# Linear attention with an expert-choice MLP: how 12 of 16 blocks of normed rows are turned

## Chip, cores and metric

The kernel runs on one core of one Trainium2 chip. Its time is device microseconds (us) from start to end of one execution; lower is better. Below, "rows" are tokens, "turned" means transposed.

## What is computed

x is (2, 4096, 512), fp32. Cut to what matters:

```python
xn = layernorm(x)                          # per row of 512
q, k, v = split(xn @ W_qkv + b_qkv)        # 16 heads of 32 columns
q, k = relu(q), relu(k)                    # times cos and sin of the position
kv   = einsum('bhld,bhle->bhde', k_cos, v) # and the same for sin
ctx  = (q_cos @ kv_cos + q_sin @ kv_sin) / (norm + 1e-4)
attn = ctx @ W_out + b_out
probs = softmax(xn @ choice_w.T)           # 8 experts, each takes its best 1024 rows of a batch
ffn  = scatter_add(gain * (silu(rows @ w1[e]) @ w2[e]))   # rows = the chosen rows of xn
out  = x + attn + ffn
```

## The kernel before

The program is written engine by engine; each engine runs its own list in order, and semaphores tie them together. SP (SyncE) issues nearly all loads and stores. There are three stages.

**Projections**, twice (once per batch), 8 blocks of 512 rows each, in four tiles (t) of 128 rows. For block n, VectorE (DVE) norms the rows of block n + 1 in two halves of two tiles (`norm_half`, lines 690 to 724): statistics (L693 to L699), a square root on ScalarE (ACT, L508), a Newton step (L704 to L713), then L719 writes the normed rows into the buffer `xn`. SP stores them to a DRAM table `normed` (L346), from which the experts later gather rows. TensorE (PE) turns each 128x512 tile of `xn` with four 128x128 transposes into a PSUM bank (`turn_x`, L1177), ACT copies it to `xT_hi` in a rounded fp32 form (L515), and DVE subtracts to get the rest `xT_lo` (`turned_lo`, L729). Every product is three matmuls (hi\*hi, lo\*hi, hi\*lo: L1161 to L1163). PE's order in a block: the query products of 512 rows (`q_half`, `q_rest`), then for each tile the value product `v_of` (with the router's 8 columns), the key product `k_of`, and `kv`, which adds keys x values of the tile before into PSUM. The transposes of block n + 1 stand between these: tiles 0 and 3 behind `v_of`, tiles 1 and 2 behind `k_of`. DVE answers each tile with `v_out` (L871 to L884), `k_out` (L891), `turned_lo`, `k_low` (L896); ACT with `turned_hi` and `k_high` (L566).

x comes in through one buffer, `xq`, that is the upper half of `xo`; the lower half is used for the first block's second half and, in the next stage, for output tiles. So the load of a half (L305) waits until the half before has been normed.

At the start SP loads, in this order: two halves of x, two tables, the query weights, the router's rows, the value weights, biases, the key weights (L310, each 1 MB and on 128 partitions). ACT and DVE split each part in hi and lo (L539, L554; L830, L847) before they go on to the first block. After block 1's halves are stored, SP loads W_out, and GpSimd (POOL) splits it (L389, L391).

**Attention**, 32 tiles per batch, with the search for each expert's chosen rows beside it; at the end of batch 0 PE turns the four tiles of batch 1's first block. **Experts**, 8 times 4 units of 512 gathered rows: here the rows already come in pieces of 128 numbers and are turned by DVE in 32x32 blocks (`rows_turn`, L790), and w1 is loaded by four loads of 32 partitions each (L331).

Of the kernel before, what the change touches and what calls it, by code (L numbers as in the profile page):

```python
# [32 lines left out]
P = 128  # L33
# [8 lines left out]
BLK = 512  # L42
# [71 lines left out]
def build(nc, x, w_qkv, b_qkv, w_out, b_out, choice_w, w1, w2, consts, bits, out, scratch):  # L114
# [6 lines left out]
    with ExitStack() as ctx:  # L121
# [31 lines left out]
        with ExitStack() as early:  # L153
# [26 lines left out]
            probE = sb("probE", [P, E, NT])  # L180
            probT = sb("probT", [P, 2, P])
            mark = sb("mark", [P, 2, P])
# [13 lines left out]
        xq, x_first = xo[:, 2:4, :], xo[:, 0:2, :]  # L196
# [51 lines left out]
        x_in, xn_ready = sem("x_in"), sem("xn_ready")  # L248
# [44 lines left out]
        def _(sp):  # L293
# [5 lines left out]
            def store_normed(j, s):  # L299
                sp.wait_ge(xn_ready, j * TPB + (2 * s + 2))  # L300
                sp.dma_start(normed[bass.ds(j * BLK + 2 * s * P, 2 * P), :].rearrange("(t p) d -> p t d", p=P),
                             xn[:, 2 * s:2 * s + 2, :]).then_inc(xn_stored[s], 16)

            def load_x(row):
                sp.dma_start(xq, xf[bass.ds(row, 2 * P), :].rearrange("(t p) d -> p t d", p=P)  # L305
                             ).then_inc(x_in, 16)

            def load_weights(part):
                src = w_out if part == O else w_qkv[:, part * D:(part + 1) * D]
                sp.dma_start(raw_weights(part), src.rearrange("(k p) d -> p k d", p=P)).then_inc(w_in[part], 16)  # L310


            load_x(0)
            sp.dma_start(x_first, xf[2 * P:4 * P, :].rearrange("(t p) d -> p t d", p=P)).then_inc(x_in, 16)
# [3 lines left out]
            sp.dma_start(ch_rows, choice_w[:, :]).then_inc(ch_in, 16)  # L318
# [20 lines left out]
            for b in range(B):  # L339
                def next_block(nxt):  # L340
                    src = nxt * BLK
                    for s in range(2):
                        sp.wait_ge(xn_ready, nxt * TPB + 2 * s)
                        load_x(src + 2 * s * P)
                        sp.wait_ge(xn_ready, nxt * TPB + (2 * s + 2))
                        sp.dma_start(normed[bass.ds(src + 2 * s * P, 2 * P), :].rearrange("(t p) d -> p t d", p=P),  # L346
                                     xn[:, 2 * s:2 * s + 2, :]).then_inc(xn_stored[s], 16)

                if b == 0:
                    next_block(1)  # L350
                    load_weights(O)
                with sp.Fori(1 if b == 0 else 0, min(NBLK, B * NBLK - 1 - b * NBLK)) as i:
                    next_block(b * NBLK + i + 1)
# [3 lines left out]
                             prob[:, :, :]).then_inc(prob_stored, 16)  # L357
                if b == B - 1:
# [146 lines left out]
        def _(act):  # L505
# [4 lines left out]
            def turned_hi(j, t, matmuls, bank=7):  # L510

                act.wait_ge(tr_done, j * TPB + t + 1)
                if matmuls is not None:
                    act.wait_ge(mm_done, AHEAD + matmuls)
                nc.scalar.copy(xT_hi[:, :, t * P:(t + 1) * P],  # L515
                               ps[:, bank, :].rearrange("p (k c) -> p k c", k=KD)).then_inc(xT_hi_ready, 1)

# [23 lines left out]
            act.wait_ge(w_in[Q], 16)  # L541
# [10 lines left out]
            for part in (V, K):  # L552
                act.wait_ge(w_in[part], 16)
                nc.scalar.copy(wq_hi[:, :, part * D:(part + 1) * D], raw_weights(part)).then_inc(w_hi_ready, 1)  # L554
            act.wait_ge(con_in, CON_LOADS * 16)
            for b in range(B):
# [11 lines left out]
                def block(i):  # L568
# [7 lines left out]
                    for t in range(TPB):  # L576
                        turned_hi(n + 1, t, n * 12 + (2 * t + 6))
                        k_high(n, t)

# [19 lines left out]
                for t in range(TPB):  # L599
                    k_high(n_last, t)  # L600
                    if b < B - 1 and t == 0:
                        sqrt(n_last + 1, 0)
# [10 lines left out]
                if b < B - 1:  # L613
                    sqrt(n_last + 1, 1)

                def step(t, ring):
# [23 lines left out]
                    if t == 4:  # L640
                        act.wait_ge(xn_ready, min((b + 1) * NBLK * TPB + TPB, XN_TILES))
# [44 lines left out]
        def _(dve):  # L686
            me = Steps(dve, dve_steps)

            def norm_stats(j, s, src, loads):

                dve.wait_ge(x_in, loads * 16)
# [9 lines left out]
            def norm_rows(j, s, src, reuse):  # L701
# [20 lines left out]
            def norm_half(j, s, src, loads, reuse):  # L722
                norm_stats(j, s, src, loads)
                norm_rows(j, s, src, reuse)
# [100 lines left out]
            norm_half(0, 0, xq, 2, False)  # L825
            norm_half(0, 1, x_first, 2, False)
# [36 lines left out]
            for b in range(B):  # L863
# [42 lines left out]
                norm_half(n_first + 1, 0, xq, n_first * 2 + 3, True)  # L906
                tile_out(n_first, 0, 0)
                norm_half(n_first + 1, 1, xq, n_first * 2 + 4, True)
# [4 lines left out]
                with dve.Fori(0, NBLK - 2) as turn:  # L913
                    me.enter(turn, N_BLOCK)
                    n = b * NBLK + turn + 1
                    for s in range(2):
                        norm_half(n + 1, s, xq, n * 2 + (s + 3), True)
                    for t in range(TPB):
                        tile_out(n, turn + 1, t)
                    me.leave(NBLK - 2)  # L920

                n_last = (b + 1) * NBLK - 1
                for t in range(TPB):
                    if b < B - 1 and t == 0:
                        norm_stats(n_last + 1, 0, xq, n_last * 2 + 3)
# [3 lines left out]
                    if b < B - 1 and t == 0:  # L929
                        norm_rows(n_last + 1, 0, xq, True)  # L930
# [24 lines left out]
                if b < B - 1:  # L955
# [497 lines left out]
```

## Time and profile before

| | |
|---|---|
| median of 3 runs | 2461.06 us (2458.93 to 2461.28) |
| the profiled execution | 2461.76 us, its span 2459.8 us |
| PE busy | 2411.8 us, 98% of the span |
| DVE / ACT / POOL busy | 1388.7 / 678.7 / 1103.5 us |
| projections of batch 0 and 1 | about 17 to 348 us and 522 to 847 us |

The span is what the profiler sees between the first and the last instruction; the execution's own time is 2 us longer. "Busy" of PE is the time in which at least one matmul is under way; matmuls overlap, so what one costs is read from the distance of starts, not from its duration. PEclk is the granted TensorE clock as a share of 2.4 GHz.

### The profile page before, as it was taken

How to read it: one execution, taken by the hardware profiler on the slowest of the kernel's cores; microseconds unless marked ns; L12 is line 12 of the kernel's file. 1: busy time of each engine (PE TensorE's matmuls, PEld its weight loads, DVE VectorE, ACT ScalarE, POOL GpSimd, SP SyncE). 2: the span in 40 equal slices, each digit the busy share in tenths (PEclk: the TensorE clock that was granted, in tenths of full speed). 3: DMA queues.
4: the chain of work that ended last, by engine and by line, in shares of the span. 5: the costliest groups of instructions: out<-in, count | busy, mean ns of one | idle time of the engine just before them, and what ended most of it. 6: DMA issues, size and time to landing. Idle time of an engine off the chain costs nothing.

```text
span 2459.8 us, 36636 instructions
## 1 busy us (share of the span) xinstructions
PE 2411.8 (98%) x13002; PEld 2051.9 (83%) x13002; DVE 1388.7 (56%) x2928; ACT 678.7 (28%) x1153; POOL 1103.5 (45%) x973
## 2 busy tenths in 40 slices
PE   7999999999999989999999999999999999999997
PEld 6999988889999878888888888888888888888886
DVE  7666678976666698834624534534543543543543
ACT  2212124432111245422322322322322322323222
POOL 1000014410000136666666566666566665665765
PEclk9999999999999999999999999999999999999999
DMA  5434335434343344632432432532522523523422
GB/s 181 114 95 105 97 67 72 56 82 103 102 102 94 60 72 66 128 83 49 88 75 50 110 55 48 111 54 45 117 51 48 118 47 48 118 46 64 104 45 43
DMA packets 101399, 197.76 MB, mean 80 GB/s; under 512 B 27032, under 2 KB 27032, under 8 KB 101024
## 3 DMA queue, kind: packets, MB, share of 16 engines
q0 software_dynamic: 57728, 119.09, 28.0%
q1 hardware_dynamic: 43552, 76.92, 10.7%
q8 instruction: 95, 1.56, 0.3%
q14 instruction: 24, 0.20, 0.0%
HBM read 111.80 MB, written 100.93 MB: 86 GB/s over the span
## 4 chain that ended last, share of the span: by engine, by line
PE 94%; DVE 5%; issue 0%; ACT 0%; DMA 0%; POOL 0%; SPq 0%; DVEq 0%; POOLq 0%; ACTq 0%
PE ps L1161 31%; PE ps L1162 30%; PE ps L1163 30%; PE ps L1370 1%; PE ps L1177 1%; DVE work L1096 1%; PE ps L1188 1%; DVE vv_lo L884 0%; DVE work L1079 0%; DVE k_lo L1086 0%; DVE thr L997 0%; DVE first_lo L751 0%; PE ps L1355 0%; DVE xn L719 0%; DVE mark L987 0%
## 5 line engine op out<-in xcount | busy, mean ns | idle before, releaser
L396 POOL DMA_INDIRECT rows<-normed_rows,idx_row x528 | 563.0, 1066 | 212.1 <-issue 212.1
L1161 PE MATMUL ps<-xi_hi,w_hi 128*128 128x512 f32 x1024 | 404.6, 395 | 0.2
L1161 PE MATMUL ps<-w_hi,h_hi 128*128 128x512 f32 x1024 | 402.3, 393 | 0.0
L1162 PE MATMUL ps<-xi_lo,w_hi 128*128 128x512 f32 x1024 | 400.3, 391 | 0.0
L1162 PE MATMUL ps<-w_lo,h_hi 128*128 128x512 f32 x1024 | 399.4, 390 | 0.0
L1163 PE MATMUL ps<-w_hi,h_lo 128*128 128x512 f32 x1024 | 399.0, 390 | 0.0
L1163 PE MATMUL ps<-xi_hi,w_lo 128*128 128x512 f32 x1024 | 398.7, 389 | 0.0
L493 POOL DMA_INDIRECT out_dram<-y,idx x128 | 221.2, 1728 | 275.7 <-ACT y L676 262.3
L1128 DVE CAST h_hi<-hf 128x512 fp32r<-128x512 f32 x256 | 111.7, 436 | 411.2 <-ACT hf L657 410.1
L657 ACT ACTIVATE hf<-ps 128x512 f32<-128x512 f32 x256 | 153.1, 598 | 509.9 <-PE ps L1163 509.8
L1161 PE MATMUL ps<-wq_hi,xT_hi 128*128 128x256 f32 (+2 forms) x768 | 248.8, 324 | 1.6 <-ACT qT L559 1.6
L1163 PE MATMUL ps<-wq_hi,xT_lo 128*128 128x256 f32 (+2 forms) x768 | 246.6, 321 | 0.0
L1162 PE MATMUL ps<-wq_lo,xT_hi 128*128 128x256 f32 (+2 forms) x768 | 245.8, 320 | 0.0
L1163 PEld LDWEIGHTS ps<-xi_hi,w_lo 128*128 128x128 f32 x1024 | 192.6, 188 | 41.1
L1163 PEld LDWEIGHTS ps<-w_hi,h_lo 128*128 128x128 f32 x1024 | 192.4, 188 | 40.6
L1161 PEld LDWEIGHTS ps<-xi_hi,w_hi 128*128 128x128 f32 x1024 | 192.2, 188 | 40.3 <-issue 1.3
L1161 PEld LDWEIGHTS ps<-w_hi,h_hi 128*128 128x128 f32 x1024 | 192.4, 188 | 39.1
L1162 PEld LDWEIGHTS ps<-w_lo,h_hi 128*128 128x128 f32 x1024 | 192.4, 188 | 38.9
L1162 PEld LDWEIGHTS ps<-xi_lo,w_hi 128*128 128x128 f32 x1024 | 192.4, 188 | 38.0
L676 ACT ACTIVATE y<-ps,gain 128x512 f32<-128x512 f32 x128 | 88.2, 689 | 456.4 <-PE ps L1163 456.4
L797 DVE TENSOR_TENSOR xi_lo<-rowsT,xi_hi 128x512 fp32r<-128x512 f32 x132 | 90.0, 682 | 210.2 <-ACT xi_hi L524 207.2
L1130 DVE TENSOR_TENSOR h_lo<-hf,h_hi 128x512 fp32r<-128x512 f32 x256 | 178.0, 695 | 8.8
(169 smaller groups left out, 4296.4 us busy)
## 6 DMA issues: line engine op xcount, KB each, us to landing
w_raw<-in_L_ffn_w_dram SPq DMA_DIRECT2D x36, 512.0 KB, 8.2
w_raw<-in_L_ffn_w_dram SPq DMA_DIRECT2D x9, 2048.0 KB, 10.4
xo<-in_L_attn_x_dram SPq DMA_DIRECT2D x32, 512.0 KB, 4.1
normed_rows<-xn SPq DMA_DIRECT2D x32, 512.0 KB, 3.0
out_dram<-bo POOLq DMA_DIRECT2D x16, 1024.0 KB, 9.2
out_dram<-xo POOLq DMA_DIRECT2D x64, 256.0 KB, 4.1
rows<-normed_rows,idx_row POOLq DMA_INDIRECT x528, 2.7
qT<-in_L_attn_W_qkv_dram SPq DMA_DIRECT2D x3, 1024.0 KB, 9.4
```

Of the source, the lines that this page charges most:

```text
L396: nc.gpsimd.indirect_dma_start(rows[:, tt, a, :], None, pieces[:, :], bass.IndirectOffsetOnAxis(ap=idx_row[:, b, tile, a:a + 1], axis=0)). ...
L493: nc.gpsimd.indirect_dma_start(of[:, :], bass.IndirectOffsetOnAxis(ap=idx[:, u * TPB + tt:u * TPB + tt + 1], axis=0), y[:, tt, :], None, c ...
L657: nc.scalar.activation(hf[:, m % 2, :], ps[:, m % 2, :], ACT.Silu).then_inc(silu_done, 1)
L676: nc.scalar.activation(y[:, tt, :], ps[:, 2 + tt % 2, :], ACT.Copy, scale=gain[:, u % 2, tt, bass.ds(e, 1)]).then_inc(y_ready, 1)
L797: nc.vector.tensor_tensor(xi_lo[:, :, sl], rowsT[:, tt % 2, :, :], xi_hi[:, :, sl].bitcast(F32), ALU.subtract).then_inc(xi_ready, 1)
L1096: nc.vector.tensor_tensor(o4, o4, r4, ALU.mult).then_inc(o_ready, 1)
L1128: me.did(nc.vector.tensor_copy(h_hi[:, m, :], hf[:, m % 2, :]))
L1130: nc.vector.tensor_tensor(h_lo[:, m, :], hf[:, m % 2, :], h_hi[:, m, :].bitcast(F32), ALU.subtract).then_inc(h_ready, 1)
L1161: nc.tensor.matmul(dst, a_hi, b_hi, start=start, stop=False, skip_group_check=True)
L1162: nc.tensor.matmul(dst, a_hi, b_lo, start=False, stop=False, skip_group_check=True)
L1163: return nc.tensor.matmul(dst, a_lo, b_hi, start=False, stop=stop, skip_group_check=True)
L1177: last = nc.tensor.transpose(ps[:, bank, k * P:(k + 1) * P], xn[:, t, k * P:(k + 1) * P], ident)
```

## The change

Twelve blocks (2 to 7 and 10 to 15) are no longer turned by PE. Their normed rows go to the DRAM table as before and are loaded back by SP, four loads per half of a block (`load_pieces`): load i takes numbers 128i to 128i + 127 of each row into 32 partitions of `xn`, so that each partition holds pieces of 128 numbers. DVE turns each tile in 32x32 blocks into `xT_raw` (`turn_pieces`), ACT copies that to `xT_hi` (`pieces_hi`), DVE subtracts (`pieces_lo`). What comes out has the 512 features in another order, so the weights and the router's rows are loaded in that order, in pieces: four loads of 32 partitions per part instead of one of 128. Blocks 0, 1, 8 and 9 are still turned by PE; for them DVE writes the normed rows twice, once with the features reordered into `xn`, once in place. x has a buffer for either half, `x_half`, normed in place; the second is free for batch 1's blocks only when the attention stage's output tiles are stored. The norms of block 8 are moved forward into block 7.

```diff
             def norm_rows(j, s, turn):
                 me.wait()
-                if reuse:
-                    dve.wait_ge(xn_stored[s], j * 16)
-                    dve.wait_ge(tr_done, j * TPB - 2 + 2 * s)
+                if turn is not None:
+                    if turn > 0:
+                        dve.wait_ge(tr_done, turn * TPB - 2 + 2 * s)
+                    for tt in range(2):
+                        nc.vector.tensor_scalar(
+                            xn[:, 2 * s + tt, :].rearrange("p (k i j) -> p i k j", k=KD, i=HPG),
+                            src[:, tt, :].rearrange("p (i k j) -> p i k j", k=KD, i=HPG), mv[:, tt, 0:1],
+                            rstd[:, tt:tt + 1], ALU.subtract, ALU.mult).then_inc(xp_ready, 1)
                 for tt in range(2):
-                    nc.vector.tensor_scalar(xn[:, 2 * s + tt, :], src[:, tt, :], mv[:, tt, 0:1], rstd[:, tt:tt + 1],
+                    nc.vector.tensor_scalar(src[:, tt, :], src[:, tt, :], mv[:, tt, 0:1], rstd[:, tt:tt + 1],
                                             ALU.subtract, ALU.mult).then_inc(xn_ready, 1)
...
+            def turn_pieces(n, turns, t):
+                dve.wait_ge(pieces_in[t // 2], (turns + 1) * (HPG * 16))
+                dve.wait_ge(mm_done, AHEAD + n * 12 + (2 * t + 6))
+                nc.vector.transpose(
+                    xT_raw.rearrange("p k (a r) -> p a k r", a=HPG),
+                    xn[:, t, :].rearrange("p (a k j) -> p a k j", a=HPG, k=KD)).then_inc(pieces_turned, 1)
+            def pieces_lo(j, t):
+                dve.wait_ge(xT_hi_ready, j * TPB + t + 1)
+                sl = slice(t * P, (t + 1) * P)
+                nc.vector.tensor_tensor(xT_lo[:, :, sl], xT_raw, xT_hi[:, :, sl].bitcast(F32),
+                                        ALU.subtract).then_inc(xT_ready, 1)
...
+                for i in range(HPG):
+                    sp.dma_start(raw_weights(part)[i * HD:(i + 1) * HD, :, :],
+                                 w_qkv[i * P:(i + 1) * P, part * D:(part + 1) * D].rearrange("(k j) d -> j k d", j=HD)
+                                 ).then_inc(w_in[part], 16)
...
+                with sp.Fori(2, NBLK - 1) as i:
                     for s in range(2):
+                        store_normed(n + i, s)
+                        next_pieces(n + i, s)
+                        next_x(n + i + 1, s)
...
                 n_last = (b + 1) * NBLK - 1
+                if b < B - 1:
+                    norm_half(n_last + 1, 0, 2)
                 for t in range(TPB):
...
                     if b < B - 1 and t == 0:
-                        norm_rows(n_last + 1, 0, xq, True)
+                        norm_stats(n_last + 1, 1)
+                    if b < B - 1 and t == 1:
+                        norm_rows(n_last + 1, 1, 2)
...
-                    if t == 2 and b < B - 1:
-                        norm_rows(n_last + 1, 1, xq, True)
```

How the instructions move, at three places. The first is DVE in the loop over blocks, from the key product's bias to the next tile's value product (REGISTER_ALU and ISA rows set up waits and addresses; `route` holds `xT_raw`). Before:

```order
L891 TENSOR_TENSOR work<-ps,bk 128x512
L727 REGISTER_ALU
L729 TENSOR_TENSOR xT_lo<-ps,xT_hi 128x4x128
L895 REGISTER_ALU
L896 SCALAR_TENSOR_TENSOR k_lo<-work,k_hi 128x512
L870 REGISTER_ALU
L871 TENSOR_TENSOR work<-ps,bv 128x4x128
```

and of the change:

```order
L956 TENSOR_TENSOR work<-ps,bk 128x512
L779 REGISTER_ALU
L781 STREAM_TRANSPOSE route<-xn 128x4x4x32
L960 REGISTER_ALU
L961 SCALAR_TENSOR_TENSOR k_lo<-work,k_hi 128x512
L786 ISA
L788 TENSOR_TENSOR xT_lo<-route,xT_hi 128x4x128
L935 REGISTER_ALU
L936 TENSOR_TENSOR work<-ps,bv 128x4x128
```

One instruction more per tile, and the subtraction for `xT_lo` now stands behind that for `k_lo`.

The second is SP's queue at the start, from the query weights to the first load for a later block. Before:

```order
L310 DMA qT<-in_L_attn_W_qkv_dram 128x4x512
L318 DMA work<-in_L_ffn_choice_w_dram 8x512
L310 DMA qT<-in_L_attn_W_qkv_dram 128x4x512
L321 DMA bq<-in_L_attn_b_qkv_dram 128x4x1
L323 DMA bk<-in_L_attn_b_qkv_dram 128x512
L323 DMA bv<-in_L_attn_b_qkv_dram 128x512
L325 DMA bo<-in_L_attn_b_out_dram 128x512
L310 DMA qT<-in_L_attn_W_qkv_dram 128x4x512
L301 DMA normed_rows<-xn 128x2x512 x2
L305 DMA xo<-in_L_attn_x_dram 128x2x512
```

and of the change:

```order
L323 DMA qT<-in_L_attn_W_qkv_dram 32x4x512 x4
L335 DMA work<-in_L_ffn_choice_w_dram 8x4x32 x4
L323 DMA qT<-in_L_attn_W_qkv_dram 32x4x512 x4
L340 DMA bq<-in_L_attn_b_qkv_dram 128x4x1
L342 DMA bk<-in_L_attn_b_qkv_dram 128x512
L342 DMA bv<-in_L_attn_b_qkv_dram 128x512
L344 DMA bo<-in_L_attn_b_out_dram 128x512
L323 DMA qT<-in_L_attn_W_qkv_dram 32x4x512 x4
L304 DMA normed_rows<-xo 128x2x512 x2
L308 DMA xo<-in_L_attn_x_dram 128x2x512 x2
L320 DMA qT<-in_L_attn_W_out_dram 128x4x512
```

The key weights are the last part in both, W_out now comes right behind the loads of x for block 1, where it stood behind the stores of block 1 before.

The third is DVE at the start, where it norms the second half of block 0 and turns to the weights. Before:

```order
L713 TENSOR_TENSOR rstd<-rstd,newt 128x2
L719 TENSOR_SCALAR xn<-xo,mv,rstd 128x512 x2
L830 TENSOR_TENSOR wq_lo<-qT,wq_hi 128x4x128
L729 TENSOR_TENSOR xT_lo<-ps,xT_hi 128x4x128 x2
L837 TENSOR_TENSOR wq_lo<-ps,wq_hi 128x4x8
```

and of the change:

```order
L759 TENSOR_TENSOR rstd<-rstd,newt 128x2
L765 TENSOR_SCALAR xn<-xo,mv,rstd 128x4x4x32 x2
L770 TENSOR_SCALAR xo<-xo,mv,rstd 128x512 x2
L895 TENSOR_TENSOR wq_lo<-qT,wq_hi 128x4x128
L794 TENSOR_TENSOR xT_lo<-ps,xT_hi 128x4x128 x2
```

Two more writes of normed rows stand ahead of the weights, as in each half that PE turns (blocks 0, 1, 8 and 9).

## Rows read from the trace of the kernel before

**Rows 1.** The page, busy time of each engine: us, share of the span, instructions.

```profile
PE 2411.8 (98%) x13002; PEld 2051.9 (83%) x13002; DVE 1388.7 (56%) x2928; ACT 678.7 (28%) x1153; POOL 1103.5 (45%) x973
```

**Rows 2.** Timeline of PE, block 2, tile 0: start, us, engine, line, operation.

```profile
121.28 0.60 PE L1177 MATMUL ps<-con,xn 128*128 128x128 f32 x4
121.64 0.48 PE L1161 MATMUL ps<-wq_hi,xT_hi 128*128 128x512 f32 x1
121.95 0.39 PE L1162 MATMUL ps<-wq_lo,xT_hi 128*128 128x512 f32 x1
122.18 0.40 PE L1163 MATMUL ps<-wq_hi,xT_lo 128*128 128x512 f32 x1
```

**Rows 3.** By tile, `xn` and `rowsT`: duration ns min/median/max, first and last start.

```profile
L1177 PE MATMUL ps<-con,xn x256: 270/273/474, 10.6 to 806.6; 128*128 128x128 f32 x128
...
L790 DVE STREAM_TRANSPOSE rowsT<-rows x132: 667/705/715, 947.8 to 2436.0; 128x512 f32<-128x512 f32 x132
```

**Rows 4.** Timelines of DVE and PE, block 2: wait for x, and the last tile.

```profile
115.55 1.29 DVE L693 BATCH_NORM_STATS2 stats<-xo 128x6 f32<-128x512 f32 x2 [4.74 <-DMA xo<-in_L_attn_x_dram]
...
142.65 0.69 DVE L871 TENSOR_TENSOR work<-ps,bv 128x512 f32<-128x512 f32 x1 [2.36 <-PE ps L1163]
...
145.86 0.69 DVE L891 TENSOR_TENSOR work<-ps,bk 128x512 f32<-128x512 f32 x1
...
147.25 0.69 DVE L896 SCALAR_TENSOR_TENSOR k_lo<-work,k_hi 128x512 fp32r<-128x512 f32 x1
...
148.51 0.28 PE L1161 MATMUL ps<-vv_hi,k_hi 128*128 128x260 f32 x1
```

**Rows 5.** The page, DMA issues: KB each, median us from issue to landing.

```profile
xo<-in_L_attn_x_dram SPq DMA_DIRECT2D x32, 512.0 KB, 4.1
normed_rows<-xn SPq DMA_DIRECT2D x32, 512.0 KB, 3.0
...
qT<-in_L_attn_W_out_dram SPq DMA_DIRECT2D x1, 1024.0 KB, 6.1
```

**Rows 6.** Timelines of DVE, ACT and PE at the start.

```profile
13.94 1.00 DVE L719 TENSOR_SCALAR xn<-xo,mv,rstd 128x512 f32<-128x512 f32 x2
...
18.07 3.71 ACT L554 CAST wq_hi<-qT 128x2048 fp32r<-128x2048 f32 x2
...
21.00 0.40 PE L1161 MATMUL ps<-xT_hi,wq_hi 128*128 128x512 f32 x1
```

**Rows 7.** Windows while query weights and w1 load: last three PEclk, DMA share, GB/s.

```profile
10.00:11.00 1.00, 0.38 (x2) 0.41 (x3) 1.00 (x3) 0.00 (x0) 0.00 (x0) 1.00 1.03 377
...
862.00:870.00 8.00, 7.55 (x44) 6.69 (x45) 7.16 (x22) 2.99 (x6) 2.23 (x2) 1.00 1.04 204
```

**Rows 8.** Timelines of DVE, POOL, PE in block 0, and a window behind it.

```profile
48.27 7.45 DVE L884 SCALAR_TENSOR_TENSOR vv_lo<-work,con,vv_hi 128x520 fp32r<-128x520 f32 x2
...
50.27 4.89 POOL L391 TENSOR_TENSOR wo_lo<-qT,wo_hi 128x2048 fp32r<-128x2048 f32 x1
...
57.06 1.09 PE L1177 MATMUL ps<-con,xn 128*128 128x128 f32 x4 [3.54 <-DVE xT_lo L729]
...
57.00:63.00 6.00, 5.94 (x17) 4.88 (x18) 3.65 (x7) 0.00 (x0) 1.39 (x1) 0.51 0.27 99
```

**Rows 9.** Timelines of DVE and PE, attention stage of batch 0, tiles 2 and 3.

```profile
367.37 2.70 DVE L719 TENSOR_SCALAR xn<-xo,mv,rstd 128x512 f32<-128x512 f32 x2
...
372.07 0.36 PE L1161 MATMUL ps<-vv_hi 128*128 128x264 f32 x1 [0.86 <-DVE work L1079]
...
375.41 0.66 PE L1370 MATMUL ps<-con,work 128*128 128x128 f32 x4 [1.52 <-DVE work L1096]
```

**Rows 10.** Timelines of ACT, DVE and PE: a table load, and block 8.

```profile
348.48 1.28 ACT L508 ACT_TABLE_LOAD   x1
...
546.51 0.68 DVE L871 TENSOR_TENSOR work<-ps,bv 128x512 f32<-128x512 f32 x1
...
547.86 0.28 PE L1161 MATMUL ps<-wq_hi,xT_hi 128*128 128x256 f32 x1
```

More of the change, by code:

```diff
@@ L317, in _ @@
             load_weights(Q)
-            sp.dma_start(ch_rows, choice_w[:, :]).then_inc(ch_in, 16)
+            with nc.allow_non_contiguous_dma("router rows in the order of the pieces"):
+                for k in range(KD):
+                    sp.dma_start(ch_rows[:, k * P:(k + 1) * P].rearrange("e (i j) -> e i j", j=HD),
+                                 choice_w.rearrange("e (i k j) -> e k i j", i=HPG, k=KD)[:, k, :, :]
+                                 ).then_inc(ch_in, 16)
             load_weights(V)
@@ L357, in _ @@
                              prob[:, :, :]).then_inc(prob_stored, 16)
+                if b < B - 1:
+                    for s in range(RES):
+                        sp.wait_ge(out_stored[s], (b + 1) * (NT // RES) * 16)
+                    next_x(n + NBLK + 1, 1)
                 if b == B - 1:
@@ L916, in _ @@
                     for s in range(2):
-                        norm_half(n + 1, s, xq, n * 2 + (s + 3), True)
+                        norm_half(n + 1, s)
                     for t in range(TPB):
-                        tile_out(n, turn + 1, t)
+                        v_out(n, (turn + 1) * TPB + t, t, 2 * t + 5)
+                        k_out(n, t, 2 * t + 6)
+                        turn_pieces(n, b * (NBLK - 2) + turn, t)
+                        k_low(n, t)
+                        pieces_lo(n + 1, t)
                     me.leave(NBLK - 2)
                 n_last = (b + 1) * NBLK - 1
+                if b < B - 1:
+                    norm_half(n_last + 1, 0, 2)
                 for t in range(TPB):
-                    if b < B - 1 and t == 0:
-                        norm_stats(n_last + 1, 0, xq, n_last * 2 + 3)
                     v_out(n_last, (NBLK - 1) * TPB + t, t, 2 * t + 2)
@@ L1171, in turn_x @@
             def turn_x(j, t, bank=7):
-                pe.wait_ge(xn_ready, j * TPB + (t + 1))
-                if bank == 7 and not isinstance(j, int):
+                pe.wait_ge(xp_ready, by_pe[j] * TPB + (t + 1))
+                if bank == 7 and j > 0:
                     pe.wait_ge(xT_ready, j * TPB + t)
@@ L1267, in _, with block @@
                                      skip_group_check=True)
-                with pe.Fori(0, NBLK - 1) as i:
-                    n = b * NBLK + i
+                def block(n, first):
                     pe.wait_ge(xT_ready, (n + 1) * TPB)
                     q_half(0, 5, 1)
-                    pe.wait_ge(w_ready, KD)
+                    if first:
+                        pe.wait_ge(w_ready, KD)
                     pe.wait_ge(lg_read, AHEAD + n * TPB)
@@ L1277, in _ @@
                     pe.wait_ge(k_read, AHEAD + n * TPB)
-                    if b > 0:
+                    if first and b > 0:
                         pe.wait_ge(fin, AHEAD + b * NT)
@@ L1289, in _ @@
                         v_of(t)
-                        if t in (0, TPB - 1):
+                        if first and t in (0, TPB - 1):
                             turn_x(n + 1, t)
                         if t == 0:
-                            pe.wait_ge(w_ready, KD + 2)
+                            if first:
+                                pe.wait_ge(w_ready, KD + 2)
                             pe.wait_ge(q_read, AHEAD + n * KD + 4)
@@ L1297, in _ @@
                         k_of(t)
-                        if t in (1, 2):
+                        if first and t in (1, 2):
                             turn_x(n + 1, t)
@@ L1306, in _ @@
                     kv(n, TPB - 1)
+                block(b * NBLK, True)
+                with pe.Fori(1, NBLK - 1) as i:
+                    block(b * NBLK + i, False)
                 n_last = (b + 1) * NBLK - 1
```

123 lines of the change are left out of this document (74 added, 49 removed).

## Prediction

> **What bounds the kernel now.** I read the page first. TensorE (PE) is busy for 98% of the span [rows 1], so a change earns what it takes off PE's list and what it leaves there of waits, and no more. Then PE's timeline in a block: the four transposes of a tile start at 121.28, the next product at 121.64, and its second matmul 0.31 us later, where the usual distance is 0.23 [rows 2]. Read there that the group costs 0.36 + 0.08 = **0.44 us** of PE's list, though its rows show 0.60 of duration; matmuls overlap. Last the two ends of the projections, where other engines hold PE up: the first block [rows 8], and the attention stage's first tiles [rows 9].
>
> **The sum, part by part.** It is made against the profiled execution, 2461.8 us, which is 0.7 above the median of the three runs.
>
> *Transposes off PE.* The trace has 256 transposes [rows 3]; 12 blocks x 4 tiles x 4 = 192 go, in 48 groups. 48 x 0.44 = **21.1 us off the path**. In the loop PE waits for nothing, so all of it counts if the loop stays free of waits.
>
> *The loop's cover.* DVE gets one more instruction per tile. The experts stage runs the same one, same shape, in 0.705 us [rows 3]. The tight place is the last tile of a block, where the `kv` products of tile 3 wait for `k_low`. In the trace `v_out` starts at 142.65 and takes 3.12 us of work when it need not wait, `k_out` follows at 145.86, `k_low` starts at 147.25 and ends at 147.94, PE starts those products at 148.51 [rows 4]. With the group of transposes gone, PE ends `k_of` 0.44 earlier behind `v_of`; the DVE work between does not shrink, so relative to PE `k_out` slips by 0.3. The turn (0.70 instead of the old subtraction's 0.61, which moves behind) and the wait for ACT put `k_low`'s end 0.3 later, relative to PE, than before: about 0.2 us ahead of PE. The last subtraction ends near 148.9 on this scale and is needed only when the next block's second query half starts, some 1.1 us later. Tiles 1 and 2 have over 1 us of idle DVE each. I take 0 for the loop, at worst 0.3 per block.
>
> *The pieces' way.* Normed rows go out in 3.0 us and would come back in about the 4.1 that a load of x takes [rows 5]; 7.1 us. The first half's norm is done before 115.55, where the second's begins [rows 4], and the turn waits for the first key product, which starts at 121.64 [rows 2] and takes 12 x 0.23 = 2.8: at least 8.9 us. Cost 0. The 4.7 us for which DVE waited for the second half of x [rows 4] vanish, and are worth 0: PE did not wait for it.
>
> *The start, DVE.* Two halves each get two more writes of 512 numbers; two of them take 1.00 us [rows 6]. Half 0's stand before half 1's norms, half 1's before the weights' split, and PE starts on both: **+2.0 us**.
>
> *The start, loads.* This is the price the diff does not show. The query weights, one load over 128 partitions, moved at 377 GB/s. The only loads of 32 partitions in the trace, those of w1 in four parts, moved at 204 GB/s, with the DMA engines just as full (share 1.04) [rows 7]. Query, value and key parts are 3.15 MB: 8.3 us at the one rate, 15.4 at the other, so the key weights land 7.1 us later. Now ACT takes value and key parts back to back from 18.07 to 21.78 [rows 6], so the key part is there just in time at 19.9; after, ACT takes it from 27.0 to 28.9 and behind it reads out the first query product, until 29.6. PE needs that bank for its third query product: the second starts at 21.00 [rows 6] and takes 2.8, plus the 2.0 above, so 25.8. PE idles **3.8 us** (0 if the rate stays, 4.5 if small packets slow it more). A pause of 3.54 us in the trace was followed by 6 us at 0.51 of the clock [rows 8], the lower level of 1.2 GHz: 2.9 us of work lost. I charge that too: 6.7 in all.
>
> The Trainium skill, "SBUF — State Buffer", section "Door 1: The DMA port swizzle", says that a transfer into 32 partitions reaches 8 of the 16 ports, with an asymptote near 218 GB/s, and so speaks against cutting the loads this way. By that figure, as an estimate, the three parts take 14.4 us, and the sum would come out 1.0 us lower.
>
> *The start, POOL.* Before, POOL split W_out just as DVE was at `vv_lo` (a cast up to 50.27, then 4.89 us); that pair of DVE operations, which the 3.12 us of a whole `v_out` bound, took 7.45 us, and PE idled 3.54 us and lost the clock [rows 8]. That cost 6.4 us and goes away at its old place. But W_out is now asked for right behind x: key bytes end near 25, stores and x take until about 30, W_out lands 6.1 us later [rows 5], so POOL works from about 36 to 43. In that time, behind the fourth query product (about 38), DVE gets the deviations of block 1 and has a chain of tiny operations to do, which two operations of POOL hold up just as they held `vv_lo`. PE needs the result at about 39.9 and gets it at 44.4: 4.5 us, and the clock again, **7.4**. Block 0 together: 6.7 + 7.4 - 6.4 = **+7.7**. Bounds: 0.3 if neither pause comes (and then the old one's 6.4 is a gain), 18 if both last the clock's 6 us and more.
>
> *Block 8.* It is turned by PE too. Its ACT loads the square root's table again, which in the trace costs 1.28 us in the attention stage of batch 0 [rows 10] and now comes between the last query product and the deviations, with PE's transposes waiting behind them: 1.1, the 1.28 less some slack. Then the two extra writes per half: tile 1's `v_out` starts at 546.51, 0.7 before its bank was needed at 547.86 [rows 10]; 1.0 + 1.0 more of DVE ahead of it gives a wait of 1.5. Together **+2.6**.
>
> *The moved norms.* In the attention stage the norm of block 8's second half goes. It took 2.70 us there plus a chain of 1.0, and PE idled 0.86 and 1.52 us just behind [rows 9]: **-2.4** (0 to -3.7). In block 7 the same work plus its extra write stands ahead of tile 2: at most the 1.0 of that write can show, I take **+0.5**.
>
> *SP's queue.* Eight small loads more per block, each issued in well under 1 us, ahead of the next load of x. That load now has a block's time. 0.
>
> Sum: -21.1 + 2.0 + 7.7 + 2.6 - 2.4 + 0.5 = **-10.7**, so 2451.1 for the profiled execution, 2450.4 against the median. I say **2450.5 us**.
>
> **The rivals.** *One collision or none at the start.* W_out's split falls between DVE operations, or the key weights' rate holds. For it: what blocks DVE is a matter of a few us of phase. Against: POOL's window is 6.8 us long and DVE's chain 1 us, so it is hard to miss. With one of the two pauses short enough to keep the clock and be half as long, 7 less: about 2443.5; with both gone 2437.
>
> *The start costs more.* If both pauses stay and reach 6 us each, or ACT's late start spreads to the first `v_out`, 8 us more: 2458.5, within noise of no change.
>
> *Slower: the turn in the loop.* DVE's last tile has 0.2 us to spare ahead of the `kv` products of tile 3. If the turn takes longer than in the experts stage, every us beyond 0.2 costs 12 us in all, since it falls on 12 block ends and earlier tiles absorb theirs. The sum's 10.7 are used up at 1.1 us more, a turn of 1.8 us; at 2.4 us the kernel takes about 2459, and if PE's waits grew there to where the clock falls, 2475 and more. Against it: 132 turns of this shape lie between 0.667 and 0.715 [rows 3].
>
> *The change does less than it says.* Pieces that arrive too late in each block would hold the turn. There are 8.9 us for 7.1 of way; at 204 GB/s [rows 7] a half's 0.52 MB takes 2.6 us, inside those 4.1. What they were late would show as a wait of DVE first, and a us of it is again worth 12.
>
> **How the numbers follow.** A measurement of this kernel can tell 0.2%, 4.9 us, from no change. The forecast, with its terms' bounds, 0.52 (2446 to 2456); less trouble at the start 0.24 (2436 to 2446); more trouble at the start 0.16 (2456 to 2463); the loop slower 0.06, other 0.02. The range for 8 in 10 leaves out the ends of the second case and the slow loop: 2440 to 2461. Faster by over 0.2% is below 2456.1: 0.76. Slower by over 0.2% is above 2466: the slow loop and a tail of the third case, 0.07. The rest, 0.17.
>
> **What would show it.** Right: 64 transposes left on PE; the distance from one block's query products to the next's shorter by 1.75 us in blocks 1 to 6 and 9 to 14; no wait of PE on `k_lo` there. The weights' loads show near 204 GB/s between 8 and 25 us, and PE waits for `qT` at about 26. A second wait of PE before 45 us, for `xn`, while POOL splits W_out and one tiny DVE operation shows some us; the granted clock near 0.5 behind either. PE waits twice in block 8, and one table load stands there. The two waits of tiles 2 and 3 in the attention stage of batch 0 are gone. Wrong: a PE wait that comes back in each block, on `k_lo` or `xT_lo`; a rate near 377 for the cut loads; or PE never waiting before 60 us.

## The result, and the profile after

The kernel after takes 2475.66 us (median of 4 runs, 2471.53 to 2478.17) beside 2460.52 for before: ratio 1.006, 95% interval 1.0047 to 1.0072. It is **slower by 0.6%**, where 2450.5 us and a gain were forecast. The profiled execution took 2476.08 us, its span is 2474.3.

One point on the time line splits the difference: PE's first attention product of batch 1, with which the projections are over.

| | span | that product starts at | from there to the end |
|---|---|---|---|
| before | 2459.8 | 851.27 | 1608.5 |
| after | 2474.3 | 840.09 | 1634.2 |

The rows of that product, of before and of after (the columns are start, us, engine, line, operation, and in brackets the idle time ahead and what ended it):

```profile
851.27 0.36 PE L1161 MATMUL ps<-vv_hi 128*128 128x264 f32 x1 [0.77 <-issue]
...
840.09 0.36 PE L1227 MATMUL ps<-vv_hi 128*128 128x264 f32 x1 [0.77 <-issue]
```

Up to there the change gains 11.2 us, against the 10.7 of the sum. Behind it, in work that the change does not touch, 25.7 us are lost. Three more profiles of after's program (the runs with empty instructions below) have the product at 839.57 to 840.73 and 1631.7 to 1631.9 us behind it, one more of before's has 848.78 and 1608.5. So the loss is 23 to 26 us, and the gain ahead of it 8 to 12.

**The projections.** PE's timeline of after at the start:

```profile
14.96 0.59 PE L1283 MATMUL ps<-con,work 8*128 8x8 f32 x4 [3.42 <-DMA work<-in_L_ffn_choice_w_dram]
...
17.68 0.55 PE L1227 MATMUL ps<-xT_hi,wq_hi 128*128 128x256 f32 x1 [0.24 <-DVE xT_lo L794]
...
22.54 0.40 PE L1227 MATMUL ps<-xT_hi,wq_hi 128*128 128x512 f32 x1
...
29.06 0.79 PE L1227 MATMUL ps<-xT_hi,wq_hi 128*128 128x512 f32 x1 [3.57 <-ACT qT L605]
...
45.04 1.12 PE L1243 MATMUL ps<-con,xn 128*128 128x128 f32 x4 [4.75 <-DVE xn L765]
...
77.31 0.40 PE L1227 MATMUL ps<-xT_hi,wq_hi 128*128 128x512 f32 x1
...
116.89 0.40 PE L1227 MATMUL ps<-xT_hi,wq_hi 128*128 128x512 f32 x1
```

and the same product of blocks 1 and 2 in before:

```profile
68.73 0.40 PE L1161 MATMUL ps<-xT_hi,wq_hi 128*128 128x512 f32 x1
...
110.06 0.40 PE L1161 MATMUL ps<-xT_hi,wq_hi 128*128 128x512 f32 x1
```

Both waits that were forecast are there. The last two rows of after are one block apart: 39.58 us, where before has 41.33. That is 1.75 less in each of 12 blocks, with no wait between. What held PE at 45.04 stands in the timelines of DVE and POOL of after:

```profile
38.26 0.17 DVE L750 RECIPROCAL rstd<-std 128x2 f32<-128x2 f32 x1 [4.97 <-ACT std L549]
38.46 1.15 DVE L753 TENSOR_TENSOR newt<-rstd 128x2 f32<-128x2 f32 x1
...
39.84 4.37 DVE L757 TENSOR_SCALAR newt<-newt 128x2 f32<-128x2 f32 x1
...
37.71 1.90 POOL L430 CAST wo_hi<-qT 128x2048 fp32r<-128x2048 f32 x1 [28.54 <-DMA qT<-in_L_attn_W_out_dram]
39.69 4.50 POOL L432 TENSOR_TENSOR wo_lo<-qT,wo_hi 128x2048 fp32r<-128x2048 f32 x1
```

A DVE operation on two numbers takes 4.37 us there and 0.17 elsewhere, while POOL splits W_out from 37.71 to 44.19. The two DVE operations that are held end with POOL's operations, at 39.61 (POOL 39.61) and 44.21 (POOL 44.19). The reciprocal at 38.26, under POOL's first, is not held. The windows of after (PE, PEld, DVE, ACT, POOL busy, then PEclk, DMA share, GB/s) show the loads' rate and the granted clock behind the two waits:

```profile
12.00:16.00 4.00, 1.04 (x7) 1.02 (x8) 3.42 (x14) 2.21 (x6) 0.00 (x0) 1.00 1.07 206
...
20.00:25.00 5.00, 5.00 (x30) 4.30 (x30) 2.92 (x3) 0.91 (x1) 0.00 (x0) 1.00 1.07 218
...
28.00:32.00 4.00, 2.94 (x7) 2.36 (x8) 2.86 (x4) 1.59 (x3) 0.00 (x0) 0.50 0.69 200
32.00:36.00 4.00, 4.00 (x13) 3.15 (x13) 1.16 (x5) 0.69 (x1) 0.00 (x0) 0.67 0.88 322
...
45.00:49.00 4.00, 3.96 (x13) 3.35 (x14) 3.96 (x9) 0.00 (x0) 0.00 (x0) 0.59 0.36 133
```

**The experts' stage.** PE's busy share has fallen from 98% [rows 1] to 97%, on the page of after:

```profile
PE 2402.1 (97%) x12810; PEld 2037.9 (82%) x12810; DVE 1421.0 (57%) x2992; ACT 678.5 (27%) x1153; POOL 1101.2 (45%) x973
...
q14 instruction: 62, 0.50, 0.1%
...
PE 89%; DVE 5%; issue 3%; ACT 1%; DMA 0%; SPq 0%; DVEq 0%; POOL 0%; ACTq 0%; POOLq 0%
```

The same two lines of the page of before are:

```profile
q14 instruction: 24, 0.20, 0.0%
...
PE 94%; DVE 5%; issue 0%; ACT 0%; DMA 0%; POOL 0%; SPq 0%; DVEq 0%; POOLq 0%; ACTq 0%
```

The chain of waits has 3% of "issue" that before lacks, and q14, a queue that brings instructions, moves 62 packets (0.50 MB, so some 8 KB each) instead of 24. From 1100 us on the trace of after has these waits (us in total, times, longest), none of which before has:

```profile
DVE h_hi L1194 <- issue: 16.8, 7, 2.6
DVE w_lo L1200 <- issue: 15.7, 5, 3.5
...
PE ps L1254 <- DVE one_lo L816: 17.5, 7, 3.7
```

Seven is the number of times that the loop over the 8 experts jumps back. Here is one such place in DVE's timeline, and then what PE does there:

```profile
1190.62 1.29 DVE L847 TENSOR_TENSOR w_lo<-w_raw,w_hi 128x512 fp32r<-128x512 f32 x2 [3.55 <-ACT w_hi L566]
1194.38 0.43 DVE L1194 CAST h_hi<-hf 128x512 fp32r<-128x512 f32 x1 [2.46 <-issue]
...
1196.50 0.69 DVE L1196 TENSOR_TENSOR h_lo<-hf,h_hi 128x512 fp32r<-128x512 f32 x1
1200.10 0.69 DVE L1200 TENSOR_TENSOR w_lo<-w_raw,w_hi 128x512 fp32r<-128x512 f32 x1 [2.90 <-issue]
```

```profile
1205.09 0.36 PE L1254 MATMUL ps<-pay,one_lo 128*128 128x16 bf16 x8 [1.75 <-DVE one_lo L816]
...
1388.04 0.36 PE L1254 MATMUL ps<-pay,one_lo 128*128 128x16 bf16 x8 [3.69 <-DVE one_lo L816]
```

DVE stands twice with nothing to wait for that the profile shows: at the loop's first operation, and again behind five operations. In all seven turns the stops are at these two places; in two of them the profile puts the second one, 4.6 us, down to ACT's `w_hi`. DVE does not catch up before PE needs `one_lo`. The windows of after behind the waits give the clock:

```profile
1206.00:1210.00 4.00, 4.00 (x21) 2.97 (x19) 3.97 (x7) 0.08 (x1) 3.08 (x4) 0.65 0.21 54
...
1388.00:1392.00 4.00, 3.96 (x20) 3.10 (x20) 3.93 (x7) 0.00 (x0) 3.33 (x3) 0.71 0.22 54
```

The seven waits are 17.5 us; the other 8.2 of the 25.7 are 1.2 per turn, of the size of what these clocks cost (0.35 x 4 us = 1.4 behind the first wait, 0.29 x 4 = 1.2 behind the other).

### The profile page after: what moved, and what is told of

The parts are those of the page before. It is cut to its first block, busy times and chain, and to the rows that moved or that the text cites. A ratio compares the mean times of both kernels' runs of the same rounds, so it can differ in the third digit from the quotient of the medians.

```text
span 2474.3 us, 36442 instructions
## 1 busy us (share of the span) xinstructions
PE 2402.1 (97%) x12810; PEld 2037.9 (82%) x12810; DVE 1421.0 (57%) x2992; ACT 678.5 (27%) x1153; POOL 1101.2 (45%) x973
## 4 chain that ended last, share of the span: by engine, by line
PE 89%; DVE 5%; issue 3%; ACT 1%; DMA 0%; SPq 0%; DVEq 0%; POOL 0%; ACTq 0%; POOLq 0%
PE ps L1227 29%; PE ps L1228 29%; PE ps L1229 29%; PE ps L1442 1%; PE ps L1254 1%; DMA qT<-in_L_attn_W_qkv_dram 0%; DVE work L1164 0%; DVE work L1147 0%; DVE h_hi L1194 0%; DVE thr L1065 0%; DVE one_lo L816 0%; DVE w_lo L1200 0%; DVE k_lo L1154 0%; DVE first_lo L816 0%; PE ps L1427 0%
```

## The experiments

**Theory A:** the change puts 26 more DVE instructions ahead of the expert loop (the built program of DVE grew from 1756 to 1782). The loop's place in the code decides whether it is loaded again in each turn; that makes DVE late. **Theory B:** something else that the change alters (buffers, DMA traffic, another engine's code) does it.

### Empty instructions: four runs that tested nothing

```diff
+                    if b == B - 1 and t < NT:
+                        for _ in range(n * (t + 1) // NT - n * t // NT):
+                            apart(dve)
```

> The kernel before, with 20 empty instructions spread over VectorE's attention loop of batch 1 and nothing else changed; with them VectorE's loop over the experts starts as many instructions late as in the kernel after. Theory A (the position of that loop decides, since its instructions are loaded again in each turn): about 25 us slower than the kernel before, some 2485 us, with PE waiting 2 to 4 us for one_lo at seven turns and some 60 packets in the instruction queue q14. Theory B (the buffers, the DMA traffic or the code of another engine decides): the time of before, 2460 us, and 24 packets in q14.

> The kernel after, with 108 empty instructions spread over VectorE's attention loop of batch 1: 20 + 108 = 128 instructions, or one packet of 8192 B if an instruction has 64 B, so that the expert loop starts at the place within a packet that it has in before. Theory A: the waits of the experts' stage are gone and the forecast of the projections comes out, 2450 us. Theory B: the time of after, 2475 us.

Measured: `b_nops20` 0.9997 of before (0.9988 to 1.0006), `a_nops108` 1.0052 (1.0038 to 1.0065). Two more variants of after, with 20 and 64 of them, took 2474.45 and 2473.49 us. Read as they stand these refute theory A. But the profile of `b_nops20` has 36636 instructions, as before has, and those of the three variants of after have 36442, as after has. The built DVE programs are as long as without the edit too: the empty instructions were dropped. What follows is only that the medians of before and after repeat within 0.1%.

### The same with real instructions

```diff
+        spare = keep("spare", [P, n])
...
+                    if b == B - 1 and t < NT:
+                        for i in range(n * t // NT, n * (t + 1) // NT):
+                            nc.vector.tensor_copy(spare[:, i:i + 1], con[:, 0:1])
```

> The empty instructions of the four runs before were dropped when the programs were built (the profiles of the three variants of after have the same number of instructions), so they tested nothing. Here 26 real ones are added to the kernel before: copies of one column, spread over VectorE's attention loop of batch 1, which have slack there. In the built programs VectorE's body of the expert loop is 287 instructions long and lies at 1457 to 1744 in before, at 1483 to 1770 in after, and at 1483 to 1770 here. Theory A (the position of the loop in the code decides whether it is loaded again in each turn): some 2485 us, 25 us over before; about 67 packets of 8192 B in q14, five in each expert turn, and PE waiting 2 to 4 us for one_lo at seven turns. Theory B (buffers, DMA traffic, the code of another engine): 2460 us and 30 such packets.

> The kernel after with 32 such copies at the same place: VectorE's expert loop lies at 1515 to 1802. If a packet of 8192 B holds 128 instructions of 64 B, the body (287) touches three packets or four, and four for 31 of 128 positions; before is not among them and after is, so 32 further on is free of it whatever the offset. Theory A: the experts' stage runs as in before, about 2450 us, the forecast of the projections (10 us under before), and 30 to 32 packets. Theory B: 2475 us.

> The kernel after with 128 such copies: VectorE's expert loop lies at 1611 to 1898, one packet further than in after, so at the same place within a packet. Theory A with packets of 128 instructions: as slow as after or some us slower, 2475 to 2480 us, with five packets in each expert turn. If it is the number of instructions ahead of the loop that counts, or anything that any added copy undoes: 2450 us. Theory B: 2475 us.

These three ran on a chip on which before itself took 2770 us, so only ratios and packets count. Ratios to before: `b_copies26` 1.0071 (1.004 to 1.0102), `a_copies32` 0.9951 (0.993 to 0.9973); `a_copies128`, one run, 2776.34 beside 2770.02. The signs are theory A's, and q14 moved 60 packets in `b_copies26`, 26 in `a_copies32`, 62 in `a_copies128`. Only copies on DVE differ between these kernels and their bases, so q14 brings DVE's instructions. The expectations had four to seven packets more in each count; what a reload adds is as they said. The last one carries the most: 128 instructions further on, the trouble is back. The first two were repeated for their size.

> The kernel before with the 26 copies once more: on the chip of the last three runs all kernels, before too, took 2750 to 2790 us at a clock of 0.95, so that only the packets and the ratios could be read there. Theory A (position of VectorE's expert loop): 20 to 27 us over before, 2480 to 2487 us, with seven waits of PE for one_lo. Theory B: 2460 us.

> The kernel after with the 32 copies once more. Theory A: the experts' stage takes what it takes in before (1608 us from the first attention product of batch 1 to the end, 1634 in after), and the whole 2449 to 2452 us: the forecast's sum for the projections. Theory B: 2475 us.

Measured beside a before of 2459.39 us: `b_copies26_again` 2481.47 us, ratio 1.0092 (1.0076 to 1.0108), inside the 20 to 27 us expected; `a_copies32_again` 2449.97 us, ratio 0.9958 (0.9945 to 0.9972). The kernel before, its work unchanged but for 26 tiny copies, shows on its page and in its waits from 1150 us on the same trouble:

```profile
q14 instruction: 60, 0.49, 0.1%
...
PE 89%; DVE 6%; issue 3%; ACT 0%; DMA 0%; DVEq 0%; POOL 0%; ACTq 0%; SPq 0%; POOLq 0%
...
DVE w_lo L1138 <- issue: 22.4, 7, 3.5
...
DVE h_hi L1132 <- issue: 16.2, 7, 2.4
...
PE ps L1192 <- DVE one_lo L752: 14.1, 7, 2.5
```

and the kernel after with 32 of them has none of it; its page, and DVE's first work in a turn:

```profile
q14 instruction: 26, 0.21, 0.0%
...
PE 94%; DVE 4%; DMA 1%; SPq 0%; issue 0%; ACT 0%; POOL 0%; DVEq 0%; POOLq 0%; ACTq 0%
...
1196.72 0.43 DVE L1198 CAST h_hi<-hf 128x512 fp32r<-128x512 f32 x1 [0.87 <-ACT hf L702]
1197.18 0.69 DVE L1200 TENSOR_TENSOR h_lo<-hf,h_hi 128x512 fp32r<-128x512 f32 x1
```

| | first attention product, batch 1 | from there to the end |
|---|---|---|
| `b_copies26_again` | 849.51 | 1628.7 |
| `a_copies32_again` | 840.14 | 1609.2 |

The trouble can be given to before (+20.2 us behind the mark) and taken from after (-25.0), and the projections stay as they were. Theory B falls.

### Which places are bad

A DVE instruction is 64 B in the built program (after's has 1782 in 114048 B), and q14's packets are some 8.2 KB (60 in 0.49 MB); 8192 B hold 128. The body of the expert loop has 287, counted with the label that it jumps back to.

> The kernel before with 26 copies inside VectorE's expert loop, behind the outputs of its third unit of work, where VectorE has slack; the loop starts at instruction 1457 as in before and ends at 1770 as in after. Theory A in its sharper form (what counts is whether the body lies in three packets of 8192 B or reaches into a fourth): the end decides, so PE waits for one_lo at the start of seven turns again, about 22 us over before as in b_copies26_again, with five packets in each turn. Rival (where the body starts decides): no reloading, and the 26 copies of about 0.06 us, 8 times, lie in VectorE's idle time: 2460 us and 30 packets.

> The kernel after with 14 copies ahead of VectorE's expert loop (body at 1498 to 1784). In the trace of after VectorE stands a second time ahead of w_lo of the second tile, which is instruction 1503 of the built program; if a packet ends there (some 1500 to 1503), its neighbours end about 128 further on each time, at 1630, 1758 and 1886. Then this body still begins in the packet that ends at 1502 and ends behind 1758, in a fourth: theory A gives five packets in each turn, near 2475 us, with the second stop ahead of the first tile's work already.

> The same with 22 copies (body at 1506 to 1792): eight instructions further, behind the packet's end at about 1502, so the body lies in three packets. Theory A: no reloading, 30 to 32 packets, about 2450 us. If the end of a packet is elsewhere, both this run and a_copies14 go the same way.

> The kernel before with the longer body once more, beside a before of about 2460 us. Its body begins 44 instructions ahead of the packet's end (19 in after), and in its trace VectorE's first stop was 2.5 us as in after and the second only 0.35 us. Theory A: five packets in each turn, and a loss below that of b_copies26_again (22 us): 3 to 12 us. Rival (the body's start decides): no loss.

The edit of `b_longer26` puts the copies into the body instead:

```diff
+                    if u == UNITS - 2:
+                        for i in range(26):
+                            nc.vector.tensor_copy(spare[:, i:i + 1], con[:, 0:1])
                     rows_turn(n + 1, 0)
```

These four fell on the chip at 2770 us again (2756.79 and 2755.66 for the two variants of after, beside 2771.05). The packets of q14 on their pages settle the matter. All variants together, instructions counted from 0:

| kernel | body of the expert loop, instructions | q14 packets | reloaded |
|---|---|---|---|
| before | 1458 to 1744 | 24 | no |
| `b_copies26` | 1484 to 1770 | 60 | yes |
| after | 1484 to 1770 | 62 | yes |
| `b_longer26` | 1458 to 1770 | 60 | yes |
| `a_copies14` | 1498 to 1784 | 26 | no |
| `a_copies22` | 1506 to 1792 | 26 | no |
| `a_copies32` | 1516 to 1802 | 26 | no |
| `a_copies128` | 1612 to 1898 | 62 | yes |

One rule fits all eight: **a body that lies in three packets stays, one that reaches into a fourth is loaded again in every turn**. For the eight counts to come out, a packet must end behind one of the instructions 1488 to 1497: before, which ends at 1744, is free, and so is `a_copies14`, which begins at 1498. DVE's second stop in after narrows it down. It lies between `h_lo` of the second tile, instruction 1495, and `w_lo`, 1497, so the end is behind 1495 or 1496, and others follow 128 further on each time, behind 1623, 1751 and 1879 or one later. Of 128 starts 30 are bad (an expectation says 31). The expectation for `a_copies14` was wrong because it took `w_lo` for instruction 1503. That it is the body's end that decides, `b_longer26` shows: it begins where before does.

It also shows that a reload can cost next to nothing: 1.0026 of before (1.0007 to 1.0044), and 1.0008 (0.9992 to 1.0024) in the repeat, where 22 us and then 3 to 12 us were expected. `b_copies26` on a chip of the same speed, with the same 60 packets, took 1.0071. DVE's timeline of `b_longer26` behind a jump:

```profile
1458.34 0.43 DVE L1129 CAST h_hi<-hf 128x512 fp32r<-128x512 f32 x1 [2.49 <-issue]
...
1468.41 0.42 DVE L1129 CAST h_hi<-hf 128x512 fp32r<-128x512 f32 x1
```

The first stop is as long as in after. The second row is instruction 1495, at the packet's end. DVE gets there 10.1 us behind the first stop and does not stop; in after it gets there 2.8 us behind it (1194.38 to 1197.2) and stands for 2.90. Two `one_lo` are written before that point, and PE has no wait for `one_lo` in this trace. So the likely reason for the low cost is that the next packet has time to arrive, but no run varies that distance alone. This was seen only on the slower chip, whose traces have "issue" stops at many other places too; the cost on the other was not measured.

### The two costs at the start

For `a_kw`, on top of the 32 copies:

```diff
-            for part in (V, K):
-                act.wait_ge(w_in[part], HPG * 16)
+            part_high(V)
             act.wait_ge(con_in, CON_LOADS * 16)
...
                     q_out(n, 0, 1, 6, 2)
+                    if n == 0:
+                        part_high(K)
...
                     sqrt(n + 1, 0)
+                    if n == 0:
+                        act.wait_ge(w_in[O], 16)
+                        nc.scalar.copy(wo_hi[:, :, :], raw_weights(O)).then_inc(wo_hi_ready, 1)
...
                     small_tables()
+                    dve.wait_ge(wo_hi_ready, 1)
+                    nc.vector.tensor_tensor(wo_lo[:, :, :], raw_weights(O), wo_hi[:, :, :].bitcast(F32),
+                                            ALU.subtract).then_inc(wo_ready, 1)
```

and POOL's two operations on W_out go; `a_k` has only the part on K.

> The kernel after with 32 copies and two of its costs at the start taken away: ScalarE turns to the first two outputs of Q before it rounds the K weights, which land late, and the split of W_out is taken from POOL and given to ScalarE (high part) and VectorE (low part, behind the small tables). In the trace of after PE waits 3.57 us at 29.06 behind the K weights and 4.75 us at 45.04 behind VectorE, which stood at operations of 2 numbers while POOL split W_out. The forecast's terms: 3.8 + 2.9 (clock) = 6.7 for the first, 4.5 + 2.9 = 7.4 for the second. If these are right and nothing comes late in their place: 14 us under a_copies32_again, 2436 us. Rival: the clock is low in this stretch anyway, so only the waits come back, 8 us: 2442 us. Rival: VectorE is full in block 0, and the first wait's place is taken by one for the load or the norms: 2446 us.

> As a_kw, with the change to the K weights alone; W_out is split by POOL as in after. If the two costs are independent: 6 to 7 us under a_copies32_again, 2444 us. If VectorE, held by POOL until 44.2 us, sets the end of this stretch whatever comes before it: no change, 2450 us, and PE's wait for xn grows from 4.75 to about 8 us.

Measured: `a_k` 2445.56 us (0.9943 of before, 0.9928 to 0.9958), `a_kw` **2440.25 us, 0.992 of before (0.9907 to 0.9934)**. The first attention product of batch 1 starts at 835.03 and 829.92, after 840.14 in `a_copies32_again`: 5.1 us for each part; the medians differ by 4.4 and 5.3. In PE's timeline of `a_k` the wait for K is gone, and the one behind POOL has another victim:

```profile
45.76 0.79 PE L1235 MATMUL ps<-wq_hi,xT_hi 128*128 128x512 f32 x1 [4.48 <-DVE work L961]
```

since in DVE's timeline of `a_k` it is now two writes of 520 columns that are held up (POOL splits W_out from 36.74 to 43.35), which take 0.89 us in `a_kw`:

```profile
36.93 6.70 DVE L950 TENSOR_SCALAR vv_hi<-work,con 128x520 fp32r<-128x520 f32 x2
```

In PE's timeline of `a_kw` this is what is left:

```profile
34.76 0.66 PE L1252 MATMUL ps<-con,xn 128*128 128x128 f32 x4 [0.27 <-DVE xn L768]
...
47.65 0.36 PE L1236 MATMUL ps<-wq_hi,xT_hi 128*128 128x256 f32 x1 [1.90 <-DVE logit L943]
```

A full DVE takes part of the second cost's place, as one rival said (1.90 us of wait at 47.65), and the 9.7 us that came back in all (2449.97 to 2440.25) lie between the forecast's 14 and the 8 of the waits alone. For `a_k`, 2444 us were expected if the costs are independent and 2450 if not: 2445.56 is near the first. Each part gives back 5.1 us up to the mark, less than the 6.7 and 7.4 charged; that is net of the work that the second part puts on ACT and DVE, so it does not measure the two terms by themselves. In `a_kw` the granted clock stays at 1.00 from 20 to 60 us. `a_kw` beats both kernels.

## Why the prediction was wrong

**The step that failed is the sum itself: it ends with the projections.** It has no term for the experts' stage. Each DVE instruction that the change adds was charged its duration; its place in the code was taken to be worth nothing. It was worth 25.7 us: the body's end moved from instruction 1744 to 1770, past the end of a packet at 1751 or 1752. The rival for "slower" looked for a loss in the projections' loop, which has no wait at all. The trace of before could have raised the question but not answered it: q14 moves its last packet there in the first turn of the expert loop, between 1196 and 1200 us, so the later turns run on what stays; how little there was to spare, seven or eight instructions, no row says.

With the loop moved out of the way `a_copies32_again` was profiled at 2451.09 us; the sum said 2451.1. That the two agree so closely is partly luck, as the steps show. By the sum's own steps, read in the traces of before and after:

- *Transposes, the loop's cover, pieces, SP's queue:* right. 1.75 us a block, 12 times, is 21.0 (21.1 said). No PE wait in the loop.
- *The start, DVE:* the two extra pairs of writes took 2.0, as charged, but the first product came only 0.8 later, at 17.68 instead of 16.88. The first half of x landed 1.1 us earlier, which the sum did not have (5.6 to 5.9 in after and all its variants, 6.8 to 7.3 in before and its variants; why is not shown). At the second query product it is +1.5 (22.54, before 21.00 [rows 6]). The first rows of DVE, before and after:

```profile
6.82 1.28 DVE L693 BATCH_NORM_STATS2 stats<-xo 128x6 f32<-128x512 f32 x2 [6.82 <-DMA xo<-in_L_attn_x_dram]
...
5.68 1.29 DVE L738 BATCH_NORM_STATS2 stats<-xo 128x6 f32<-128x512 f32 x2 [5.68 <-DMA xo<-in_L_attn_x_dram]
```

- *The start, loads:* right. Wait 3.57 (3.8 said); clock 0.50 from 29.06 to 32 and 0.67 to 36, 2.8 lost (2.9 said). The cut loads moved 206 and 218 GB/s in the windows shown, so the trace agrees with the Trainium skill, "SBUF — State Buffer", section "Door 1: The DMA port swizzle", on 32 partitions.
- *The start, POOL:* right in place and size. POOL from 37.7 to 44.2 (36 to 43 said), the wait for `xn` 4.75 (4.5); the clock cost less behind it, 1.6 against 2.9. Start and block 0 together: 77.31 against 68.73, **+8.6**, where 2.0 + 7.7 = 9.7 were said. The parts read here, 1.5 + 3.6 + 2.8 + 4.8 + 1.6 - 6.4, make 7.9; a wait of 0.3 at 57.8 is part of the rest, and 0.4 is not assigned. The 6.4 for the old pause is what one execution shows. In `b_nops20`, whose program is before's, POOL begins its split 1.4 us later (49.66, before 48.28), PE's pause is 1.80 instead of 3.54, and the granted clock stays at 1.00 behind it.
- *Block 8:* one wait of 0.99 for `xn` (1.1 said) and one of 1.08 (1.5); the whole block takes 2.5 longer (2.6 said). *Moved norms:* of 0.86 and 1.52 [rows 9] only 0.31 is left in after, -2.1 (-2.4 said).
- *Block 7:* +0.9 instead of +0.5: after is ahead by 1.96 us where the block starts and by 1.05 at batch 0's first attention product (350.79, before 351.84). It is not the extra write. PE has no wait on DVE there, but an "issue" stop of 0.77 ahead of that product, which before does not have. The rows of PE's timeline of after:

```profile
350.79 0.36 PE L1227 MATMUL ps<-vv_hi 128*128 128x264 f32 x1 [0.77 <-issue]
...
370.56 0.36 PE L1227 MATMUL ps<-vv_hi 128*128 128x264 f32 x1 [0.31 <-DVE work L1147]
...
535.12 0.66 PE L1243 MATMUL ps<-con,xn 128*128 128x128 f32 x4 [0.99 <-DVE xn L765]
...
547.15 0.36 PE L1227 MATMUL ps<-wq_hi,xT_hi 128*128 128x256 f32 x1 [1.08 <-DVE logit L940]
```

Together 8.6 - 21.0 + 0.9 - 2.1 + 2.5 = -11.1, and -11.2 are measured. So each of the forecast's costs up to the mark is there, and the misses at the start and in block 7 partly offset each other.

Two figures beside the sum do not follow from it. The bound "0.3 if neither pause comes" is what is left when only the second stays away (6.7 - 6.4); with neither it is -6.4. And by the prediction's own rule, 12 us for each us beyond 0.2, a turn of 2.4 us gives 18 us and 2468.5, not 2459.

The jumps back show as stops of 2.3 to 2.6 us, with nothing else to wait for. On them bears the Trainium skill, "Runtime: NRT & Kernel Launch", section "Instruction fetch mechanics": code is streamed by blocks into a small memory, and a taken branch whose target is no longer in it waits for a fetch; the trace agrees. It does not agree on the sizes. The section gives two blocks of 16 KiB, 256 instructions each. With these the bad places would come again every 256 instructions, and after and `a_copies128`, 128 apart, could not both be bad; they are, and the packets measure some 8.2 KB (60 in 0.49 MB), of which three stay. The measurement decides.

## What to carry to other kernels

A hardware loop whose body nearly fills the packets of code that stay can fall out of them when instructions are added anywhere ahead of it on its engine. So count, for each engine with a long loop, where the body begins and ends, and compare the instruction queues' packets on the page before and after a change: a count that grows with the turns, with "issue" waits at the loop's first operations and another engine's waits behind them, names the cause. The count alone does not: `b_longer26` has it at hardly any cost. Where the packets end cannot be read from the program; here it took runs at several positions. A few tiny real instructions ahead of the loop move it; empty ones were dropped here. The two fixes at the start gave back 5.1 us each where 6.7 and 7.4 were charged, so measure such fixes one at a time.

## What was not expected

- DVE's code comes in packets of 128 instructions; a body in three stays, one that reaches into a fourth costs five packets a turn, one more than it touches, and stops of 2.3 to 4.6 us (`a_copies14` against after: 14 instructions decide 36 packets).
- The cost of a reload hangs on where it falls: 25.7 us in after, hardly anything in `b_longer26`, with 62 and 60 packets.
- SP took 3.03 us to issue the four small loads of the router's rows, and PE stood for them until 14.96; it had no term in the sum. In after the wait cost nothing, since PE's first product still waited for DVE behind it; in `a_copies32_again` it lasted until 16.22, and the first product came at 18.36.
- The DVE operations that POOL holds up have no length of their own: 4.37 us for two numbers in after, 6.70 for two writes of 520 columns in `a_k`. In after they end when POOL's operation ends, and an operation between them, at 39.65, takes 0.16.
